# Local attention layers of a transformer on one core: the layers' weights, q/k scale rows and rotary table handled once per layer instead of once per round

## What is computed

```python
DIM, DEPTH, HEADS, DIM_HEAD, WINDOW = 128, 6, 16, 64, 32
def attn_layer(x, Wqkv, qs, ksc, Wo):
    q, k, v = split(x @ Wqkv)                   # 16 heads of 64
    q = l2norm(q) * qs; k = l2norm(k) * ksc     # one scale row each per layer
    q = q * cos * scale + rotate_half(q) * sin * scale
    k = k * cos / scale + rotate_half(k) * sin / scale
    return local_attention(q, k, v) @ Wo        # windows of 32, looks one window back
for i in range(DEPTH):
    x = attn_layer(shift_tokens(x), Wqkv[i], q_scale[i], k_scale[i], Wo[i]) + x
    x = ffn_layer(shift_tokens(x), ln_g[i], ln_b[i], W1[i], b1[i], W2[i], b2[i]) + x
```

## Time and profile before

| | us |
|---|---|
| median of three runs | 4658.14 |
| the three runs | 4657.95, 4658.14, 4670.21 |
| the profiled execution | 4670.98 |
| span in the profiled execution | 4669.2 |

### The profile page before, as it was taken

One profiled execution on the slowest core, in us unless ns is written; L12 is line 12 of the kernel. 1 busy time (PEld: TensorE's weight loads), 2 busy tenths in 40 slices (PEclk: granted clock), 3 DMA queues, 4 the chain that ended last, 5 costly groups with the idle time before them and its releaser, 6 DMA issues. The chain is left out here.

```text
span 4669.2 us, 162098 instructions
## 1 busy us (share of the span) xinstructions
PE 4135.5 (89%) x67078; PEld 2766.5 (59%) x67078; DVE 2915.5 (62%) x4217; ACT 2616.0 (56%) x4417; POOL 2805.6 (60%) x3584
## 2 busy tenths in 40 slices
PE   5879788689999999999999999999999999999994
PEld 2434344346666666666666666666666666666663
DVE  5565656466666666666666666666666666666664
ACT  2545353446666656656656566566665656656552
POOL 0000000177777777777777777777777777777771
PEclk8989798889999999999999999999999999999997
DMA  0000000112222222222222223222222222222223
GB/s 28 3 15 2 15 2 15 41 39 65 65 70 74 58 68 67 72 55 67 66 70 64 56 68 79 62 59 70 68 72 55 65 66 70 64 56 67 70 64 81
DMA packets 284568, 258.77 MB, mean 55 GB/s; under 512 B 122871, under 2 KB 258508, under 8 KB 271148
## 3 DMA queue, kind: packets, MB, share of 16 engines
q1 hardware_dynamic: 283820, 248.14, 20.0%
HBM read 117.63 MB, written 29.77 MB: 32 GB/s over the span
## 5 line engine op out<-in xcount | busy, mean ns | idle before, releaser
L787 DVE TENSOR_TENSOR products<-bank_d,table 128x1024 f32<-128x1024 f32 x772 | 938.1, 1216 | 684.4 <-ACT sq L614 679.7
L910 POOL TENSOR_TENSOR products<-products 128x2048 f32<-128x2048 f32 x192 | 871.0, 4536 | 313.8 <-DVE products L787 313.8
L413 PE MATMUL bank_d<-w_qkv,xT 128*128 128x512 f32 x1544 | 807.5, 626 | 18.7 <-issue 13.0
L614 ACT ACTIVATE sq<-bank_d 128x512 f32<-128x512 f32 x772 | 468.0, 606 | 469.9 <-PE bank_d L413 457.4
L947 POOL TENSOR_TENSOR qk_rot<-products,rnorm 128x2048 f32<-128x2048 f32 x192 | 695.6, 3623 | 14.0 <-POOL rnorm L929 12.7
L785 DVE TENSOR_REDUCE ss<-sq 128x16 f32<-128x1024 f32 x386 | 468.8, 1214 | 229.3 <-ACT sq L614 229.3
L874 POOL MEMSET ident<- 128x128 f32 x1 | 0.2, 205 | 915.1 <-POOLq L1064 915.1
L954 POOL TENSOR_TENSOR prob<-prob,inv_sum 128x1024 f32<-128x1024 f32 x192 | 365.4, 1903 | 307.3 <-DVE inv_sum L767 307.3
L1491 DVE TENSOR_REDUCE part_max<-s_max 128x1 f32<-128x512 f32 (+3 forms) x768 | 399.5, 554 | 152.2 <-PE s_max L1240 101.3
L478 PE MATMUL scores<-kT,qT 64*32 64x64 f32 x24576 | 430.4, 218 | 24.4 <-issue 24.4
L413 PE MATMUL bank_a<-w_qkv,xT 128*128 128x512 f32 x768 | 403.1, 607 | 49.7 <-ACT gate L669 47.5
(11 more groups left out here) (168 smaller groups left out, 7581.9 us busy)
## 6 DMA issues: line engine op xcount, KB each, us to landing
v_back<-v SPq DMA_DIRECT2D x96, 768.0 KB, 5.4
w_qkv<-in_Wqkv_dram SPq DMA_DIRECT2D x25, 1024.0 KB, 5.1
v_back<-v SPq DMA_DIRECT2D x192, 128.0 KB, 5.7
w_qkv<-in_Wqkv_dram SPq DMA_DIRECT2D x25, 512.0 KB, 5.4
xs<-x_layers SPq DMA_DIRECT2D x194, 64.0 KB, 2.1
w_o<-in_Wo_dram SPq DMA_DIRECT2D x24, 512.0 KB, 6.9
xr<-x_layers SPq DMA_DIRECT2D x96, 128.0 KB, 3.0
x<-x SPq DMA_DIRECT2D x96, 128.0 KB, 1.8
```

Source lines behind the costliest of these rows:

```text
L413: nc.tensor.matmul(bank[:, :], xT[:, P * a:P * (a + 1)], w_qkv[:, col:col + 512], start=True, stop=True).then_inc(d_filled if i < 8 else a ...
L614: nc.scalar.activation(sq[j % 2][:, 8 * c:8 * c + 8, :], bank_d[slot][:, :].rearrange("p (h d) -> p h d", d=DH), ACT.Square).then_inc(squa ...
L787: nc.vector.tensor_tensor(products[:, a, head:head + 8, :, :].rearrange("p h r (o d) -> p h r o d", o=2), bank[:, :].rearrange("p (h r d) ...
L910: link(nc.gpsimd.tensor_tensor(products[:, a, :, 0, :], products[:, a, :, 0, :], products[:, a, :, 1, :], ALU.add))
```

## The change

The step objects now carry the layer, the sequence `b` and the position `p` apart. The loads of `w_qkv`, `w_o` and the feed-forward weights are issued in one round of four, and so is `load_qk_rows`: `w_qkv` in the last step of the layer (b = 3, p = 3), the others in round b = 0, at the same places in their steps as before. GpSimd makes the table only in round b = 3, two tiles a step. The waits of the engines that use them stand only in the first round of a layer, or in the last step of a layer for `wqk_in`.

```diff
-                if runs(now) and s.p == 0:
-                    sp.wait_ge(table_ready, POS * (s.f + 1))
-                    load_qk_rows(s.f + 1)
-                if runs(now) and s.p == POS - 1:
+                if runs(now) and s.b == 0 and s.p == 0:
+                    sp.wait_ge(table_ready, POS * (s.layer + 1))
+                    load_qk_rows((s.layer + 1) % DEPTH)
+                if runs(now) and s.b == BATCH - 1 and s.p == POS - 1:
                     sp.wait_ge(d_filled, chunk_at(now, 7)[1] + 1)
-                    load_w_qkv(s.f + 1, 0, 2 * INNER, wqk_in)
+                    load_w_qkv((s.layer + 1) % DEPTH, 0, 2 * INNER, wqk_in)
...
-                if runs(back2) and s.p == 1 and in_rounds(s):
+                if runs(back2) and s.b == 0 and s.p == 1 and in_rounds(s):
-                    load_wo(s.f)
+                    load_wo(s.layer)
...
-                    if s.p == POS - 1:
+                    if s.b == BATCH - 1 and s.p == POS - 1:
-                        load_w_qkv(s.f + 1, 2 * INNER, 3 * INNER, wv_in)
+                        load_w_qkv((s.layer + 1) % DEPTH, 2 * INNER, 3 * INNER, wv_in)
...
-                    if s.p == 2 and in_rounds(s):
+                    if s.b == 0 and s.p == 2 and in_rounds(s):
-                        load_ffn(s.f)
+                        load_ffn(s.layer)
...
-                    if s.p == POS - 1:
-                        pe.wait_ge(wqk_in, 16 * (s.f + 2))
+                    if s.b == BATCH - 1 and s.p == POS - 1:
+                        pe.wait_ge(wqk_in, 16 * (s.layer + 2))
...
-                if i == 8 and s.p == 0:
-                    pe.wait_ge(wv_in, 16 * (s.f + 1))
+                if i == 8 and s.b == 0 and s.p == 0:
+                    pe.wait_ge(wv_in, 16 * (s.layer + 1))
...
-                if s.p == 2:
-                    pe.wait_ge(wo_in, 16 * (s.f + 1))
+                if s.b == 0 and s.p == 2 and in_rounds(s):
+                    pe.wait_ge(wo_in, 16 * (s.layer + 1))
...
-                    if s.p == 3:
-                        pe.wait_ge(wffn_in, 64 * (s.f + 1))
+                    if s.b == 0 and s.p == 3:
+                        pe.wait_ge(wffn_in, 64 * (s.layer + 1))
...
-                    dve.wait_ge(table_ready, pair.n + 1)
+                    dve.wait_ge(table_ready, POS * pair.layer + pair.p + 1)
...
-                    make_table(s.f + 1, s.p)
+                    if s.b == BATCH - 1:
+                        make_table(s.layer + 1, s.p)
```

More of the change, by code:

```diff
@@ L101, with __init__ @@
 class Step:
-    def __init__(self, f, p):
-        self.f, self.p = f, p
-        self.t = POS * f + p
+    def __init__(self, layer, b, p):
+        self.layer, self.b, self.p = layer, b, p
+        self.f = BATCH * layer + b
+        self.t = POS * self.f + p
     def pair(self, lag):
@@ L119, in __init__ @@
         self.f = step.f + q // POS
+        self.layer = step.layer + (step.b + q // POS) // BATCH
         self.n = step.t - lag
@@ L123, in __init__ @@
         self.exists = not isinstance(self.n, int) or 0 <= self.n < PAIRS
-def layer_of(f):
-    return (f // BATCH) % DEPTH
 def dram_rows(region, f, row, count):
@@ L242, in rounds @@
                 for p in range(POS):
-                    step_fn(Step(b, p))
+                    step_fn(Step(0, b, p))
             with nc.Fori(1, DEPTH, engines=[eng.engine], hint_back_edge=True) as layer:
@@ L246, in rounds @@
                     for p in range(POS):
-                        step_fn(Step(BATCH * layer + b, p))
+                        step_fn(Step(layer, b, p))
             for t in range(PAIRS, PAIRS + MAX_LAG):
-                step_fn(Step(ROUNDS, t - PAIRS))
+                step_fn(Step(DEPTH, 0, t - PAIRS))
         def prev(s):
-            return Step(s.f, s.p - 1) if s.p else Step(s.f - 1, POS - 1)
+            if s.p:
+                return Step(s.layer, s.b, s.p - 1)
+            return Step(s.layer, s.b - 1, POS - 1) if s.b else Step(s.layer - 1, BATCH - 1, POS - 1)
         def chunk_at(pair, i):
@@ L278, in _, with load_w_qkv, load_qk_rows, load_wo @@
         def _(sp):
-            def load_w_qkv(f, lo, hi, done):
-                sp.dma_start(w_qkv[:, lo:hi], w["Wqkv"][bass.ds(layer_of(f), 1), :, lo:hi]
+            def load_w_qkv(layer, lo, hi, done):
+                sp.dma_start(w_qkv[:, lo:hi], w["Wqkv"][bass.ds(layer, 1), :, lo:hi]
                              .rearrange("one k n -> (one k) n")).then_inc(done, 16)
-            def load_qk_rows(f):
-                sp.dma_start(qk_row[:, :, :], w["qk_rows"][bass.ds(layer_of(f), 1), :]
+            def load_qk_rows(layer):
+                sp.dma_start(qk_row[:, :, :], w["qk_rows"][bass.ds(layer, 1), :]
                              .rearrange("one (r d) -> one r d", d=DH).to_broadcast([P, 4, DH])).then_inc(qkrow_in, 16)
-            def load_wo(f):
-                sp.dma_start(w_o[:, :, :], w["Wo"][bass.ds(layer_of(f), 1), :, :]
+            def load_wo(layer):
+                sp.dma_start(w_o[:, :, :], w["Wo"][bass.ds(layer, 1), :, :]
                              .rearrange("one (c k) n -> k (one c) n", k=P)).then_inc(wo_in, 16)
-            def load_ffn(f):
-                layer = bass.ds(layer_of(f), 1)
+            def load_ffn(layer):
+                layer = bass.ds(layer, 1)
                 sp.dma_start(w_1[:, :], w["W1"][layer, :, :].rearrange("one k n -> (one k) n")).then_inc(wffn_in, 16)
@@ L311, in _ @@
             sp.dma_start(rotary[:, :, :, :], w["rotary"]).then_inc(rotary_in, 16)
-            load_xs(Step(0, 0).pair(0))
+            load_xs(Step(0, 0, 0).pair(0))
             load_w_qkv(0, 0, 2 * INNER, wqk_in)
@@ L524, in _ @@
             pe.wait_ge(constants_ready, INIT)
-            transpose_x(Step(-1, POS - 1))
+            transpose_x(Step(-1, BATCH - 1, POS - 1))
             for i in range(EARLY):
-                project(Step(-1, POS - 1), i)
+                project(Step(-1, BATCH - 1, POS - 1), i)
             def step(s):
@@ L686, in step @@
                 if runs(back3):
-                    if s.p == 3:
-                        act.wait_ge(wffn_in, 64 * (s.f + 1))
+                    if s.b == 0 and s.p == 3:
+                        act.wait_ge(wffn_in, 64 * (s.layer + 1))
                     bank = filled(s, "xn")
@@ L725, in _ @@
             act.wait_ge(constants_ready, INIT)
-            copy_x(Step(-1, POS - 1))
+            copy_x(Step(-1, BATCH - 1, POS - 1))
             for i in range(EARLY):
-                square(Step(-1, POS - 1).pair(-1), i)
+                square(Step(-1, BATCH - 1, POS - 1).pair(-1), i)
             rounds(act, step)
@@ L829, in step @@
                 if runs(back3):
-                    if s.p == 3:
-                        dve.wait_ge(wffn_in, 64 * (s.f + 1))
+                    if s.b == 0 and s.p == 3:
+                        dve.wait_ge(wffn_in, 64 * (s.layer + 1))
                     hidden_units(s, "A")
@@ L859, in _ @@
             for i in range(EARLY):
-                rotate(Step(-1, POS - 1).pair(-1), i)
+                rotate(Step(-1, BATCH - 1, POS - 1).pair(-1), i)
             rounds(dve, step)
@@ L892, in _, with make_table @@
             pool.wait_ge(constants_ready, INIT)
-            def make_table(f, p):
-                pool.wait_ge(qkrow_in, 16 * (f + 1))
+            def make_table(layer, p):
+                pool.wait_ge(qkrow_in, 16 * (layer + 1))
                 rows = slice(2 * p, 2 * p + 2)
```

## The result

| | before | changed |
|---|---|---|
| median of 18 runs each, us | 4661.23 (4650.99 to 4678.65) | 4685.78 (4662.81 to 4703.40) |
| ratio, with its 95% interval | 1 | 1.0045 (1.0029 to 1.0060) |
| profiled execution, its span, us | 4670.98, 4669.2 | 4678.20, 4676.4 |

The changed kernel is slower by 0.45%, a little more than the 0.3% that a measurement can tell from no change. The forecast was no change. A second comparison, made with the experiments, gives 1.0042 (1.0019 to 1.0065), so the loss is small and real.

The account below looks back on a forecast made before the run. The prediction took TensorE's chain of matmuls as the bound, with holes where program fetches stand behind data. Its terms, -5 - 4.6 - 12 + 16 + 4, gave about -2 us from 4658.1: 4656, range 4628 to 4686.

Parts of the forecast that it names:

- (e): p = 2, b = 3: the border moves 11 instructions toward the edge, one step in five lost; +4 us (0 to +24).
- (d): p = 1, b = 1 and 3, ten steps: without w_o, v_back starts 0.5 us earlier and delays fetches; +16 us.
- (c): p = 0, b = 3, five steps: the fetch border falls 11 instructions later, shortening the hole; -12 us (-20 to 0).
- (b): Layer 0, p = 1: long steps shorten without the w_o load ahead of v_back; -4.6 us (-4.6 to 0).
- (a): b = 2, p = 3: two long steps shorten as their w_qkv load is gone; -5 us (-9 to 0).
- Fewer transfers, fewer holes: With w_o gone, fetches get through in all ten p = 1 steps: -41 us, 4617 us; gain over 14 us, chance 0.27.
- The v_back copy in w_o's place: Fetches at p = 1 and at p = 2, b = 3 fall behind v_back: +47 us, 4705; loss over 14, chance 0.23.
- The change does not reach TensorE: TensorE's holes are not fetches behind data and stay as they are: 0, 4658 us; chance 0.12.

Follow-up runs that it names:

- padded kernel: Changed kernel plus nine spare instructions (eighteen already met waits) on TensorE, once ahead of the layer loop, moving fetch borders back: 4661.16 us, ratio to before 0.9985.

## Why the forecast was wrong

The mechanism held (holes where a fetch stands behind the v_back copy, and borders that move with the instructions left out) and the undisturbed step too. What failed is how the move of the borders was spread over the steps. Term (e) put b = 1, p = 2 at nothing, and it came to +15.4. Term (d) did not count the move at b = 3, p = 1 at all and gave +16 for another reason; measured were +21.4 there. By the means of two profiles the five terms come to +16 where -2 was forecast; (e) is 14 of the miss and (d) 8, with 4 and 2 the other way in (c) and (b). The measured 4685.78 lies just inside the range of 4628 to 4686.

- **(a) w_qkv at b = 2, p = 3, given -5.** -9.4 against the first profile of before, 0 against the second. The hole is there in some executions only; two profiles can't fix it, and that the mean, -4.5, is as forecast is luck in part.
- **(b) w_o in layer 0, given -4.6.** -6.4 by the means, with the two profiles of before 5.3 apart. Right as far as this tells.
- **(c) p = 0, b = 3, given -12.** -15.9. Right in place too: the hole stands at L519 with 1.28 us. The new loads with the old borders left it at 208.8, so it is the borders, as said. That b = 1, p = 0 would stay at the same length was right (+1.1); the hole did move, from L445 to ahead of L412, which I had not said.
- **(d) p = 1, given +16.** The reason failed here. That the size was near (+24 for the two groups) was luck. I took the border as fixed and let w_o's absence decide. The loads alone gave some +7 in these ten steps (387.1 against a mean of 380.3); +21 of the +24 is at b = 3, where the border moved by eleven. I had counted those eleven instructions at p = 0 and at p = 2 and not at p = 1, between them. At b = 1, where steps near 41 us were given, they take 36.7 to 41.0, 39.2 by the mean, against 38.6 before. The sign that I gave for it was off as well: the wait ahead of L444 rose to 34.6 us, not 45, since b = 1 hardly changed, and that ahead of L412 rose to 17.1 instead of falling below 5, since b = 1, p = 0's hole came to stand there while b = 3's left it.
- **(e) p = 2, given +4 at b = 3 and nothing at b = 1.** +2.9 and +15.4. This is the largest miss. "Seven instructions being 0.05 us" was right for the length of p = 0, and p = 2 at b = 1 was left out of the sum without a reason. The padded kernel shows that with the new loads the move of the border brings it (back to 184.4). A move by nine under the old loads did not (184.1), so why it comes at seven, or whether it takes the new loads as well, stays open.
- **The rivals.** "Fewer transfers, fewer holes" is refuted: without moved borders the loads gave some 7 us, not 41. "The v_back copy in w_o's place" had the right sign and the right culprit, but its new place in the queue is worth a few us only (the loads alone); what matters is that a block is needed while it runs. "The change does not reach TensorE" fell.
- **The level.** I took the sum from the median of three runs, 4658.1; eighteen gave 4661.2. Worth 3 us of the miss of 30.
- **Two readings.** The 2.77 us stated for "each of ten steps" at p = 0 is that of the second layer; the ten holes are 2.2 to 3.5 us. And the 244 instructions a fetch leave out TensorE's waiting instructions; with them it is 253. Neither changes the sum.

The runs give the balance: the loads are worth about -0.15% and the borders +0.57% (1.0042 against 0.9985). The Trainium skill ("Runtime: NRT & Kernel Launch", Instruction fetch mechanics) calls a crossing "mostly hidden". With the copy late it nearly is; with the copy where it stands, it cost the two kernels over 70 us.

## What to carry to other kernels

When an engine that is busy nine tenths of the time shows holes "<-issue" at the same places in every loop, look at what the DMA engines carry a few microseconds before, and move the big transfer, not the small loads. Count the engine's instructions in program order: if the holes fall on one place of a block of fixed length, they are fetches of the program. An edit that adds or takes a few waiting instructions on that engine shifts all its later program; time it once more with spare instructions that put the borders back before you judge it. And take two profiles of each kernel where steps come in two lengths.

## What the hardware showed that I had not expected

- Nine instructions that do nothing, once per execution, were worth 20 to 27 us of 4680. Eleven fewer at b = 3, p = 1 brought holes of up to 3.3 us into five steps that had holes of up to 1.3. Two instructions off left 4 to 9 us in a group.
- 259 of 288 holes stand at one place in blocks of 256 instructions, whatever the engine is doing there.
- A hole costs more than its length. That of 2.52 us at b = 3, p = 1 came with 0.50 of the clock for over 4 us and made the stretch 6.2 us longer than an undisturbed one. That of 1.28 us at b = 3, p = 0 had 1.00 throughout and made it 1.6 longer.
- Moving the borders by half a block changed single groups by 20 to 30 us and the total by nothing (1.0048 against 1.0045).
- 247 spare instructions with 494 waits that were already met took TensorE 26.9 us, 0.11 us each.
